# Cross-attention and a routed feed-forward on one core: an expert tile listed three batches earlier, two of its quarters among the last scores

## The reference

```python
x = x + attention(layernorm(x), ctx, ctx)            # 16 heads of 16, masks, Wq, Wk, Wv, Wo, bo
def ffn(x):                                          # 8 experts, hidden 1024
    gate = softmax(x @ w_gate.T)
    top_scores, top_idx = top_k(gate, 2)
    cw = (one_hot(top_idx, 8) * top_scores[..., None]).sum(1)
    h = gelu(einsum('td,edh->teh', x, W1) + b1)
    y = einsum('teh,ehd->ted', h, W2) + b2
    return einsum('ted,te->td', y, cw)
x = x + ffn(layernorm(x))
```

## Time and profile before

| | us |
|---|---|
| median of 3 runs | 513.76 (510.2 to 513.87) |
| profiled execution | 513.29 |
| its span | 512.0 |
| TensorE busy | 456.8 (89%) |
| VectorE busy | 359.9 (70%) |
| ScalarE busy | 334.5 (65%) |
| GpSimd busy | 164.2 (32%) |

### The profile page before, as it was taken

How to read it: one execution, slowest core, us unless ns; L and a number is a source line. 1 busy time by engine, 2 the same in 40 slices (tenths; PEclk the granted TensorE clock), 3 DMA queues, 4 the chain that set the end, 5 groups by cost and what they waited for, 6 DMA issues and landing times.

```text
span 512.0 us, 10489 instructions
## 1 busy us (share of the span) xinstructions
PE 456.8 (89%) x3741; PEld 391.0 (76%) x3741; DVE 359.9 (70%) x791; ACT 334.5 (65%) x569; POOL 164.2 (32%) x213
## 2 busy tenths in 40 slices
PE   4897999999999868678899895999999999999992
PEld 3464666666765646358899895999999999999992
DVE  3367676776777863449968992688878877878862
ACT  1123776667666534449689672788879888989870
POOL 6023330352320587504425222043321213213313
PEclk9899999999999975859999988899999999999998
DMA  7666615324320032394668759687888979888922
GB/s 230 180 184 203 215 66 172 111 87 134 120 93 26 20 110 96 127 357 152 209 203 273 225 171 210 224 245 230 246 239 253 262 215 279 252 278 229 284 27 31
DMA packets 68935, 93.03 MB, mean 182 GB/s; under 512 B 6931, under 2 KB 55699, under 8 KB 68883
## 3 DMA queue, kind: packets, MB, share of 16 engines
q1 hardware_dynamic: 59648, 81.41, 49.1%
q0 software_dynamic: 7152, 9.46, 9.3%
q10 hardware_dynamic: 2080, 1.49, 1.0%
HBM read 63.01 MB, written 14.26 MB: 151 GB/s over the span
## 4 chain that ended last, share of the span: by engine, by line
PE 53%; issue 11%; ACT 9%; POOL 9%; DVE 9%; DMA 6%; SPq 2%; ACTq 1%; DVEq 0%; POOLq 0%
PE S L1221 15%; PE bank L1236 13%; PE bank L1281 6%; POOL lists L578 5%; PE bank L1289 5%; PE S L1321 4%; DVE nmax L866 3%; PE bank L1356 3%; DMA w_in<-in_W 3%; ACT hf L1071 2%; PE S L1394 2%; ACT W2p L1052 2%; PE S L1344 1%; ACT Q L1040 1%; POOL x2n L568 1%
## 5 line engine op out<-in xcount | busy, mean ns | idle before, releaser
L1221 PE MATMUL S<-xgT,Q 128*128 128x256 f32 (+1 forms) x736 | 140.2, 291 | 8.8 <-DVE xgT L760 5.3
L537 POOL DMA_INDIRECT out<-y,slot x39 | 67.1, 1721 | 182.8 <-DVE y L784 126.5
L1221 PEld LDWEIGHTS S<-xgT,Q 128*128 128x128 f32 x736 | 118.3, 199 | 9.6 <-issue 9.4
L866 DVE TENSOR_REDUCE nmax<-S 128x4 f32<-128x1024 f32 x64 | 78.4, 1224 | 47.4 <-PE S L1321 44.9
L1221 PE MATMUL S<-xgT,K 128*128 128x256 f32 (+1 forms) x368 | 106.1, 288 | 0.0
L1071 ACT ACTIVATE hf<-S,b1c 128x256 f32<-128x256 f32 (+1 forms) x184 | 70.4, 434 | 35.4 <-PE S L1221 31.6
L1146 ACT ACTIVATE prob<-S 128x1024 f32<-128x1024 f32 x64 | 65.7, 1027 | 31.0 <-PE S L1344 30.1
L737 DVE TENSOR_TENSOR K<-w_in,Q 128x1024 fp32r<-128x1024 f32 x46 | 56.4, 1225 | 26.7 <-ACT Q L1040 26.6
L770 DVE TENSOR_TENSOR hp<-hf,hp 128x512 fp32r<-128x512 f32 (+1 forms) x92 | 55.7, 606 | 27.0 <-ACT hp L1084 26.7
L1221 PEld LDWEIGHTS S<-xgT,K 128*128 128x128 f32 x368 | 73.1, 199 | 0.0
L1236 PE MATMUL bank<-W2p,hp 128*128 128x256 f32 x528 | 67.8, 285 | 0.5 <-DVE y L780 0.3
(11 more groups left out here) (179 smaller groups left out, 699.6 us busy)
## 6 DMA issues: line engine op xcount, KB each, us to landing
w_in<-in_W SPq DMA_DIRECT2D x46, 1024.0 KB, 7.2
K<-flat_k SPq DMA_DIRECT2D x24, 256.0 KB, 2.4
Q<-flat_q SPq DMA_DIRECT2D x24, 256.0 KB
xg<-lists SPq DMA_DIRECT2D x16, 265.0 KB, 5.8
b_in<-in_b SPq DMA_DIRECT2D x23, 128.0 KB, 6.0
lists<-zero SPq DMA_DIRECT2D x9, 265.0 KB, 5.7
cin<-in_ctxT SPq DMA_DIRECT2D x8, 256.0 KB, 3.8
xin<-in_x SPq DMA_DIRECT2D x8, 256.0 KB, 4.2
```

The lines of the kernel that those rows point to most:

```text
L537: st_y[i % 4].after(pool.indirect_dma_start(out=out, out_offset=bass.IndirectOffsetOnAxis(ap=slot[i % 4][:, t:t + 1], axis=0), in_=y[i % 2 ...
L866: max_done.after(dve.tensor_reduce(nmax[n % 4][:, :, :, m].rearrange("p t r -> p r t"), S1[:].rearrange("p r (t k) -> p r t k", t=TT), AX. ...
L1221: ins = pe.matmul(h_bank[pair][:, u, 0:n], W1p[k][a][:, kc, m * P:(m + 1) * P], xgT[k][c][:, kc, 0:n], start=(j == 0), stop=(j == len(term ...
```

## The change

It alters the tables of steps, and some rules with them:

- `SURE` becomes (1, 4, 2): one tile is laid out on the counts through batch 3, four on those through batch 5, two on those through batch 6. `lists_of` has a stage more, at step 59; the stages are now at 59, 69, 77 and 86 (before 70, 79 and 92). Stage 1 is now the one that runs at once.
- Units 0 and 1 run in steps 69 and 71, among the last scores, and unit 2 in step 74, unit 3 in step 75 and so on (`EARLY_UNITS`, `UNIT_STEP` = 74, `unit_of`): four steps sooner than before. The steps end at 98, so 26 units lie within them. In tile 0 the split of W1 of tile 1 and the turn of its rows move to quarters 2 and 3 (`LEAD`). Tile 0's own W1 is split in steps 66 and 67.
- Routing: batches 0 and 1 are scattered in step 50 (before 62), 2 and 3 in 58 (63), 4 in 63 (66), 5 in 69 (70), 6 in 77 (78), 7 in 87 (90). Batch 3's back part is sooner by 2 to 5 steps; others by one or two.
- Batch 7's normalisation is done on VectorE, as batch 6's was, at a step of its own (`norm_dve`).
- The empty rows are written at step 79 behind batch 6's counts, 512 rows for each list instead of 256, copied from a zeroed stretch of `lists` and not from SBUF. Batch 7's scatter waits for them.
- A tile's loads are in two parts, `sp_rows` (rows and W1) and `sp_rest` (W2 and b2), and the rows and W1 of tile i + 1 are issued ahead of W2 of tile i.
- Banks: three for small products from step 66, two from step 76. GpSimd adds tiles 0 to 3 at steps 80, 84, 89, 93.

```diff
-    SURE = (5, 2)
+    SURE = (1, 4, 2)
-    UNIT_STEP = 76
+    EARLY_UNITS, UNIT_STEP = {69: 0, 71: 1}, 74
     LATE_BACK = {
+        3: dict(div=44, divide=45, ao=46, aT=47, o=49, add=50, store=52, ln2=52, norm2=52, y=54, yT=55),
...
     LATE_ROUTE = {
+        0: dict(logits=46, choose=46, gate_exp=47, gates=48, tags=48, count=49, places=49, rows=50, scatter=50),
...
-    LISTED = {0: (3, 70), 1: (4, 79), 2: (5, 92)}
-    START, LAST = -16, 100
+    LISTED = {0: (1, 59), 1: (3, 69), 2: (4, 77), 3: (5, 86)}
+    START, LAST = -16, 98
...
-        SP_TILES = {71: (0, 1), 76: (2,), 79: (3,), 82: (4,), 86: (5,), 90: (6,)}
-        ENDS_STEP = 93
+        SP_ROWS = {62: (0,), 70: (1,), 71: (2,), 76: (3,), 78: (4,), 82: (5,), 86: (6,), 90: (7,)}
+        SP_REST = {62: (0,), 70: (1,), 75: (2,), 80: (3,), 84: (4,), 88: (5,), 92: (6,)}
+        ENDS_STEP = 79
...
         def empty_ends():
             sp.wait_ge(zrow_done.sem, 1)
+            sp.wait_ge(st_zero.sem, 2 * 16)
             for f in range(NE):
-                z = sp.value_load(zrow[0:1, f:f + 1], min_val=f * REGION, max_val=f * REGION + REGION - TS)
-                st_zero.after(sp.dma_start(lists[bass.ds(z, TS), :].rearrange("(t p) e -> p t e", p=P), zero[:]))
+                z = sp.value_load(zrow[0:1, f:f + 1], min_val=f * REGION, max_val=f * REGION + REGION - 2 * TS)
+                st_zero.after(sp.dma_start(lists[bass.ds(z, 2 * TS), :], lists[NE * REGION:, :]))
...
             def scatter(i):
                 ns = GROUPS[i]
+                if i == len(GROUPS) - 1:
+                    pool.wait_ge(st_zero.sem, 16 * (NE + 2))
...
+        def LEAD(i):
+            return 0 if i else 2
+
+        def unit_of(s):
+            return EARLY_UNITS.get(s, s - UNIT_STEP + len(EARLY_UNITS) if s >= UNIT_STEP else None)
...
         def act_unit(u):
             i, pair = divmod(u, 4)
             gelu(i, pair)
             hidden_high(i, pair)
-            if pair < 2 and i + 1 < NTILE:
-                w1_high(i + 1, pair)
             if pair >= 2:
                 w2_high(i, pair - 2)
-            if pair == 1 and i + 1 < NTILE:
+            if LEAD(i) <= pair < LEAD(i) + 2 and i + 1 < NTILE:
+                w1_high(i + 1, pair - LEAD(i))
+            if pair == LEAD(i) + 1 and i + 1 < NTILE:
                 rows_high(i + 1)
```

More of the change, by code:

```diff
@@ L286, in build @@
         st_zero, st_x2 = signal("st_zero", 16), signal("st_x2", 16)
-        st_late = [signal(f"st_late{n}", 16) for n in range(6, NB)]
+        st_late = [signal(f"st_late{n}", 16) for n in range(4, NB)]
         st_list = [signal(f"st_list{i}", 16) for i in range(KEPT)]
@@ L454, in store @@
                 sp.wait_ge(*emptied_at("o", n))
[L455 removed]
+                (st_x2 if n < 4 else st_late[n - 4]).after(sp.dma_start(out_d[n], x2[:, n * TT:(n + 1) * TT]))
             def empty_rows():
@@ L459, in empty_rows @@
                 st_x2.after(sp.dma_start(out[TRASH:, :].rearrange("(t p) e -> p t e", p=P), zero[:, :, 0:E]))
-                st_zero.after(sp.dma_start(lists[NE * REGION:, :].rearrange("(t p) e -> p t e", p=P), zero[:]))
+                for u in range(2):
+                    first_row = NE * REGION + u * TS
+                    st_zero.after(sp.dma_start(lists[first_row:first_row + TS, :].rearrange("(t p) e -> p t e", p=P), zero[:]))
             for s in range(START, LAST):
@@ L530, in add_to_output @@
             else:
-                pool.wait_ge(st_x2.sem, 16 * 7)
-            for k in range(len(SURE)):
-                if i == sum(SURE[:k + 1]):
-                    pool.wait_ge(st_late[k].sem, 16)
+                pool.wait_ge(st_x2.sem, 16 * 5)
+            for k, n in ((1, 4), (1, 5), (2, 6), (3, 7)):
+                if i == sum(SURE[:k]):
+                    pool.wait_ge(st_late[n - 4].sem, 16)
             for t in range(HT[i]):
@@ L659, in lists_of @@
                 n, start = SURE[stage], sum(SURE[:stage])
+                if stage == len(SURE) - 1:
+                    zrow_done.after(dve.tensor_tensor(zrow[:], counts, base[:], ALU.add))
                 emptied[b].after(dve.tensor_tensor(passed[:, :, 0:CHUNKS], along(counts, [P, NE, CHUNKS]),
@@ L683, in lists_of @@
                 return
-            zrow_done.after(dve.tensor_tensor(zrow[:], counts, base[:], ALU.add))
             emptied[b].after(dve.scalar_tensor_tensor(left[:], taken[:], -float(TS), counts, ALU.mult, ALU.add))
@@ L1013, in dve_attention @@
                     list_rows(now["rows"])
-                if "total" in now and now["total"] == 0:
-                    for _ in lists_of(0):
+                if "total" in now and now["total"] == 1:
+                    for _ in lists_of(1):
                         pass
@@ L1018, in dve_attention @@
                     working = lists_of(now["total"])
-                if s < UNIT_STEP:
-                    for _ in range(LIST_OPS // 2):
-                        next(working, None)
-                if s in (UNIT_STEP - 3, UNIT_STEP - 2):
-                    w1_low(0, s - UNIT_STEP + 3)
-                if s == UNIT_STEP - 1:
+                if s in (66, 67):
+                    w1_low(0, s - 66)
+                if s == 68:
                     rows_low(0)
-                if s >= UNIT_STEP:
-                    for _ in range(LIST_OPS):
-                        next(working, None)
-                    dve_unit(s - UNIT_STEP)
+                for _ in range(LIST_OPS if s >= UNIT_STEP else LIST_OPS // 2):
+                    next(working, None)
+                if unit_of(s) is not None:
+                    dve_unit(unit_of(s))
             return working
```

101 lines of the change are left out of this document (55 added, 46 removed).

## The result

The changed kernel takes 542.0 us (median of 4 runs, 540.7 to 544.2) where the kernel before takes 513.3: ratio 1.056, 95% interval 1.052 to 1.060. The prediction was 506.5 with a range of 496 to 518. It was wrong in sign and by 35 us. The first view is again the windows by stage, cut at the same steps and units as the earlier trace rows, with the steps ahead of 55 in front: up to step 54, step 54, to step 64, to step 69, to unit 4, to unit 12, to unit 28, to the end.

A forecast was written before the change was run, and what follows sets the result against it. It took the seam (184.9 to 329.8 us), where TensorE is idle or on a low clock, as the place to gain. Terms +5.5 + 3 - 7.6 - 2.3 - 0.8 - 4.6 = -6.8 from 513.3 gave 506.5 us, range 496 to 518.

The forecast's parts named there:

- A: Up to step 54: scattering batches 0 and 1 at step 50 holds TensorE; +5.5 us (0 to 7).
- Slower: Rival: the hold at step 54 drops the clock, over 12 us at low clock; 519.5 us, chance 0.17.
- B: Before step 64: 5.5 us more VectorE work into 5.8 us of room, half hidden; +3 us (0 to 5.5).
- C: Steps 64 to 68: GpSimd's queue and batch 4's routing gone, 12.5 us where it was 20.1; -7.6 us.
- D: Step 69 to unit 4: ScalarE's 26.6 us plus 3.5 us of waits; -2.3 us, stage bounds 27 to 38.
- E: Units 4 to 12: same work plus turning batch 7's sums, 30.2 against 31.0 us; -0.8 us (-2 to +3).
- F: Units 12 to 28: tile 7's rows stop waiting for the empty rows, the branch's wait stays; -4.6 us (-9 to 0).
- DMA: Around step 79: the empty rows' 19 us of queue is hidden; without cover up to 5 us.
- What would show it: Wrong if the first half of the seam (184.9 to 329.8 us) grows over 5 us, or weights wait behind empty rows.

The follow-up runs named there:

- e1: The changed kernel with the scatter of batches 0 and 1 at step 53 in place of 50: 534.4 us, ratio 1.038.
- f1: The kernel before with batches 0 and 1 chosen at step 46, counted and placed at 49, scattered at 50: 512.8 us, ratio 0.996.
- f2: The kernel before with the changed rows for batches 3 to 5 and routing of batches 0 to 5, scatter of the first two at 53: 523.2 us, ratio 1.016.
- f3: The changed kernel with batches 0 and 1 scattered at 53, tile 0's quarters from step 74, its W1, W2, b2 issued before the wait for rows: 524.3 us, 1.019.
- e2: The changed kernel with tile 0's quarters all from step 74 on and W1 of tile 1 split in quarters 0 and 1 again: 533.5 us, ratio 1.035.
- e4: The kernel before with the empty rows from batch 6's counts at step 80, batch 7's scatter behind them: 517.9 us, ratio 1.008.
- b1: The kernel before with the empty rows from batch 6's counts, issued between W1 and W2 of tile 4: 511.6 us, ratio 0.996.

## Why the prediction was wrong

**A** (+5.5): the mechanism and the wait were right (3 to 5 us forecast, 4.52 measured), the price was not. The step "TensorE is held 3 to 5 us; I take 4.5, and 1 us more" leaves out the clock behind the wait, which only the rival "Slower" had: from 168.7 to 175.5 us it was half. e1 puts the whole at 5.4 to 9 us. The rival had the sign, but its condition, more than 12 us at the low clock, did not come: it was 6.8. The other half of A, batches 0 and 1 chosen sooner, costs nothing (f1).

**B** (+3, 0 to 5.5): the step that failed is "5.5 us into a room of 5.8 that is scattered between maxima. Half hidden". It adds up VectorE's busy time and sets it against its idle time. f2 shows 2.6 us more of busy time and 8.4 us more of span, outside the range. Routing is a chain between two engines (logits, choice, count, places), and ahead of step 64 the maximum of a step stands behind it and the next scores behind the maximum. A stretch with routing takes 3.4 to 3.5 us a step there, one without it 2.3 (f1 and f2, steps 55 to 62). Behind step 64, where there are no maxima, taking batch 4's routing away gives back 1.4 us at most. The list, which the prediction named first, costs almost nothing (f3 against f2); inside it waits for nobody, which is the likely reason.

**C** (-7.6) is the term that was furthest off, 9.0 us. The step "14.7 us of matmul time is some 8.5 us at full clock ... I take 2.5 us per step: 12.5" assumed that with the queue and the routing gone nothing else would be late. f2, with just these gone, needs 14.6 us from the score of step 64 to that of 69 where f1 needs 16.0: 1.4 us was all there was to gain. In the changed kernel the wait for the maxima of batch 7 (3.34 us, 2.6 before) and the copy behind tile 0's weights (3.10 us) came on top. That the loads would now start in this stage, ahead of that copy, was not considered: what stands behind a DMA in its queues was asked for the empty rows and not for these.

**D** (-2.3, 27 to 38): ScalarE's sum was right, 26.4 us busy for a forecast of 26.6, with seven table loads. What it waits for was not, and this is the step that failed: 10.2 us in place of 3.5, so that it was busy for 72% of the stage and not for over 80. The upper bound, "each switch also waits for a unit at the low clock", is nearly what happened (36.6 us), and unit 4 waited 10.0 us for the split rows of tile 1. The early quarters did not just save little; without them, and with W1 of tile 1 split in its old place, the kernel is 8.5 to 10 us faster (e2). The loads show no drain behind them: 233.00 + 1.28 is 234.28, and the exponential starts at 234.29. By the Trainium skill (ScalarE: Activation LUTs, What ACT_TABLE_LOAD costs), which has about 1380 ns of drain at each switch, the seven would by estimate have cost 9.7 us more than they did; the trace decides against it here.

**E** (-0.8): turning batch 7's sums and dividing them comes to a wait of 3.9 us at 271.00, for the bank from which VectorE divides them into ao, at clock 0.88 over the stage. The prediction had counted the eight transposes and not who waits for what follows them.

**F** (-4.6, -9 to 0): tile 7's wait is gone and the branch's is there (2.84 us), as forecast. But "I leave that wait as it is" failed: the last list, moved by two units, now keeps VectorE at work without a pause up to 318.8, `y` stands behind it (320.51), and TensorE waits 4.62 us for it at 321.40 where it waited 2.52 for xgT. Units 20 to 28 take 28.3 us in place of 34.6, more of a gain than forecast; units 12 to 20 take 32.2 in place of 26.8 and lose nearly all of it.

**DMA**: that the empty rows are hidden held for the changed kernel. That this depends above all on SyncE's issue time (10.2 us) and not on "19 us of queue" was seen only in e4 and b1.

**The sum.** The six terms were priced one by one: B and F at the middle of their bounds, C, D and E below it, A above. All errors had one sign. I read a common cause in the runs, though none was made to show it: half-clock stretches follow many of the waits, and where two engines hand over inside a step, a new piece of work makes both wait. The range of 22 us held none of it. Even the six upper bounds together (7 + 5.5 + 0 + 5.6 + 3 + 0 = 21.1) give only 534.4 us: what was measured lies above those of A and B together, of C and of E. The last sentence of "What would show it" watched the seam's first half and 5 us: steps 64 to unit 4 grew by 5.6, just enough to trip it, but the largest growth, 19.5 us, stood ahead of the seam, where the prediction had set no such sign.

## What to carry to other kernels

Room of an engine that hands over to another at every step is not idle time less busy time: price a moved piece by the chain it opens in that step, and put it where nothing waits in turn. Before moving an early load or a batch of DMA issues, look at what small transfer or load stands behind it in each queue, on the issuing engine as much as in the DMA engines. When several terms can fail by the same cause, add their bounds with one sign, and set a sign of being wrong for every stage that gets more work, not only for the one where the gain is hoped for.
